# Second attention without the identity and bias products

## The chip, the cores and the metric

The kernel runs on one core of one Trainium2 chip. The metric is the device time of one execution in microseconds (us), less is better. TensorE, VectorE (DVE in the profile), ScalarE (ACT), GpSimd (POOL) and SyncE (SP, which only issues DMAs here) run their own instruction streams and meet at semaphores.

## The reference

Two transformer layers over x of 8 x 512 rows of 256. Each adds an attention and a mixture of experts to the rows, both from one layer norm. The first attention is a causal softmax, the second a gated linear recurrence. What matters here is the end of the second attention, `y @ Wout.T + bout`, which is added to the residual rows:

```python
xn = _layernorm(x, axis=-1)
x = x + _L1_attn_ref(xn, ...) + _L1_ffn_ref(xn, ...)

# in _L1_attn_ref
def step(M, inp):
    q_t, k_t, v_t, f_t, g_t, o_t = inp
    M = M * f_t[..., None, None] + g_t[..., None, None] * scale * (k_t[..., :, None] * v_t[..., None, :])
    y_t = jnp.einsum('bhd,bhde->bhe', q_t, M) * o_t[..., None]
    return (M, y_t)
_, yT = jax.lax.scan(step, M0, (qT, kT, vT, fT, gT, oT))
y = yT.transpose(1, 0, 2, 3).reshape(Bq, Lq, HID)
return jnp.einsum('bld,ed->ble', y, Wout) + bout
```

## The kernel before

The 4096 rows are 32 tiles of 128, kept in SBUF as `ACC` (tile i is `ACC[:, i, :]`, 128x256 f32), eight batches of four tiles. The residual rows stay in `ACC` from start to end; every part of a layer adds to them.

The work after the first layer's experts follows one written-out order, `plan2 = shared_order() + second_order()`. Each engine walks it and does the steps that have code on it. In `shared_order` the remaining products of the first layer's shared part run on TensorE (`shared_up`, L1562; `shared_down`, L1608), and `BEHIND` hangs the second layer's preparation behind them: GpSimd adds loaded sums (`sums`, L1001; `combine`, L1011), VectorE takes the statistics (`stats`), ScalarE normalizes a batch out of `ACC` into `xn1` (`norm`, which signals `xn_made`), TensorE transposes it (`xt`), ScalarE copies it out (`xa`).

`second_order` runs the second attention, one tile per turn, in the order of `ORDER1` (the first tile of each of the 8 batches, then the second of each, and so on). `TURN` gives the steps of a turn and by how many tiles each runs ahead or behind; from the 9th tile on `LATE` moves `weigh`, `out_copy` and `decay_load` to the end. Per tile n:

- TensorE: value product of the tile (`project_val`, L1753), query and key product of the next (`project_qk`, L1741), transposes (`turn`, L1769 and, from the 9th tile, L1777), state and sums of the tile before (`keys`, L1813; `update`, L1822 and L1827), affinities of the tile (`affinity`, L1795), and the output of the tile before (`project_out`).
- VectorE: state update (`update`, L2353), scan of the decays (`decay`, L2334), rotation of the next tile (`rope`, L2314; `rope_add`, L2325 and L2326), weighing of the affinities out of PSUM banks 2 to 5 (`affinity`, L2341, which signals `w_put`).
- ScalarE: values times gates (`value`, L1303), copies of the transposes (`turn`, L1310 and L1315), copy of the sums (`update`, L1321, signals `yt_put`), keys times gates (`keys`, L1339), and the copy of the output (`project_out`, L1344).
- GpSimd: opening of the gates (`open_gates`, L1030 and L1036) and the routing's scatter DMAs (L929).
- SyncE: the decays of a tile ahead (`decay_load`, L802) once `w_put` has come for the tile that held its buffer, loads of expert weights (L788), and `store_sums` (L809), a quarter of the rows at a time, once `oe_put` says that their outputs are done.

`project_val` of a tile waits for `w_put` of the tile before it on TensorE (its output shares bank 3 with the affinities). The output of a tile is made whole in PSUM bank 1: an identity matrix times the rows of `ACC` (L1836), two products of `YT` with `WOUT` (L1839), and a product of three rows of ones with the bias, split in three bf16 parts (L1840). `bias_split` (L1041 to L1055) on GpSimd prepares these parts behind `const1`. ScalarE then copies bank 1 over the rows of `ACC` and signals `oe_put`, for which the next output's first product waits. An f32 product has two records in the trace, so the 32 tiles show 64 records for L1836 and 128 for L1839.

After the last tile TensorE waits for `oe_put` and goes on to the second layer's experts; VectorE's first step there is the copy of an expert's weights (`weights`, L2186), then of the turned rows (`tile_turn`, L2174).

Of the kernel before, what the change touches and what calls it, by code (L numbers as in the profile page):

```python
# [15 lines left out]
T = NB * S  # L16
# [76 lines left out]
def attention_order():  # L93
# [10 lines left out]
    for idx in range(-LEAD, NH + 7):  # L104
# [82 lines left out]
        ("sums_copy", -1), ("project_out", -1), ("keys", 0), ("weigh", 0), ("out_copy", -1), ("rope_add", 1),  # L187
# [4 lines left out]
    (-1, "out_copy"): "scale:7 norm:7",  # L192
# [5 lines left out]
    (0, "out_copy"): "logitsT:7",  # L198
# [7 lines left out]
LATE = [s for s in TURN if s[0] not in ("weigh", "out_copy", "decay_load")] + [("weigh", 0), ("out_copy", -1), ("decay_load", 2)]  # L206
# [25 lines left out]
def second_order():  # L232
# [19 lines left out]
    out += [("rows",)] + [(kind, NT - 1) for kind in ("update", "sums_copy", "project_out", "out_copy")]  # L252
# [47 lines left out]
def build(nc, t, out):  # L300
    ctx = ExitStack()
    with ctx:
        def sem(name):
            return ctx.enter_context(nc.semaphore(name))
# [138 lines left out]
        BO3 = view(carve(128), 128, BF16)  # L443
        ones3 = view(carve(64), 64, BF16)
# [120 lines left out]
        stk_set, v_set = sem("stk_set"), sem("v_set")  # L565
# [11 lines left out]
        b_in, b_cut, b_rows, b_set = sem("b_in"), sem("b_cut"), sem("b_rows"), sem("b_set")  # L577
# [10 lines left out]
        none_set, slot_in, slot_turned, slot_off, slot_put = (sem(n) for n in ("none_set", "slot_in", "slot_turned", "slot_off", "slot_put"))  # L588
# [27 lines left out]
        out_made, oe_put, sums_out = (sem(n) for n in ("out_made", "oe_put", "sums_out"))  # L616
# [28 lines left out]
        def sync(sp):  # L645
# [50 lines left out]
            def maxrow(n):  # L696
# [3 lines left out]
                sp.wait_ge(stk_set, 3)  # L700
# [9 lines left out]
            def clear(p):  # L710
                sp.wait_ge(cst_in, 32)
                sp.wait_ge(none_set, 4)
# [41 lines left out]
            sp.wait_ge(b_cut, 5)  # L754
            sp.wait_ge(b_set, 1)
# [118 lines left out]
        def gpsimd(pool):  # L874
# [5 lines left out]
            for v in Vb:  # L880
                pool.memset(v, 0.0).then_inc(v_set)
            pool.wait_ge(v_set, 2)
            for v in Vb:
                pool.memset(v[:, :, :, 16:17], 1.0).then_inc(v_set)
            pool.wait_ge(v_set, 4)
            for n in range(3):
                if n:
                    pool.wait_ge(stk_set, n)
                pool.memset(STK[n][1][96:99, :, :].rearrange("p j s -> p (j s)").bitcast(F32), ONES2).then_inc(stk_set)
            pool.wait_ge(stk_set, 3)  # L890

            def clear_meta():
                for n, apart in enumerate((128, 0)):
                    pool.memset(unused[n][0:NTILE, :, :], 0.0).then_inc(none_set)
                    pool.wait_ge(none_set, 2 * n + 1)
                    pool.iota(unused[n][0:NTILE, :, 1], [[1, 128]], base=T, channel_multiplier=apart, allow_small_or_imprecise_dtypes=True).then_inc(none_set)
                pool.wait_ge(none_set, 4)
# [11 lines left out]
            def bias_rows():  # L909
                pool.memset(B2S, 0.0).then_inc(b_set)  # L910
                pool.wait_ge(b_in, 32)
                for k in range(3):
                    if k:
                        pool.wait_ge(b_cut, 2 * k)
                    pool.tensor_copy(b3[0:8, k, :], bstage[0:8, :]).then_inc(b_cut)
                    if k < 2:
                        pool.wait_ge(b_cut, 2 * k + 1)
# [120 lines left out]
            def bias_split():  # L1038

                pool.wait_ge(const1_set, 2)  # L1040
                pool.memset(ones3, 0.0).then_inc(const1_set)  # L1041
                for k in range(3):
                    pool.wait_ge(const1_set, 3 + k)
                    pool.memset(ones3[32 * k:32 * k + 1, :], 1.0).then_inc(const1_set)
                pool.wait_ge(const1_set, 6)
                pool.tensor_copy(BO3, BO).then_inc(const1_set)
                pool.wait_ge(const1_set, 7)
                pool.tensor_tensor(BO, BO, BO3, ALU.subtract).then_inc(const1_set)
                for k in (1, 2):
# [1422 lines left out]
```

## Time and profile before

Three runs of the kernel took 1669.58, 1671.32 and 1675.81 us. The profiled execution has a span of 1669.4 us from its first instruction to its last; its time outside the span isn't listed.

| | us |
|---|---|
| median of the runs | 1671.32 |
| span of the profiled execution | 1669.4 |
| TensorE busy | 1569.7 (94%) |
| VectorE busy | 823.6 (49%) |
| ScalarE busy | 734.2 (44%) |
| GpSimd busy | 714.7 (43%) |
| mean granted TensorE clock, share of full | 0.984 |

In time order: the first attention, the first layer's experts until about 785 us, the shared products with the second layer's preparation until about 890, the second attention until about 1131, and the second layer's experts to the end. A row of a timeline gives the start in us from the span's start, the duration in us, the engine, the line of the kernel and the operation. In brackets stands how long the engine sat idle before it and what released it. "PEld" is TensorE's weight load, which runs beside its products. "x4" at the end merges four instructions.

### The profile page before, as it was taken

The numbers are of one execution on the slowest core, as the hardware profiler recorded it, in microseconds if no ns is written. First come the engines' busy times: TensorE is split into PE (matmuls) and PEld (weight loads), VectorE is DVE, ScalarE is ACT, GpSimd is POOL, SyncE is SP. The second block draws the span as 40 slices with busy tenths as digits, with TensorE's granted clock in tenths as the row PEclk, the third lists the DMA queues.
The fourth block names the chain that finished last, engine by engine and source line by source line (L and its number), as shares of the span: only waits on it lengthen the run. The fifth ranks groups of instructions, "written<-read, shape, count | busy, mean of one in ns | idle before, by whom it ended". The sixth has DMA issues, their size and how long they took to land.

```text
span 1669.4 us, 32480 instructions
## 1 busy us (share of the span) xinstructions
PE 1569.7 (94%) x11054; PEld 1210.1 (72%) x11054; DVE 823.6 (49%) x2298; ACT 734.2 (44%) x1923; POOL 714.7 (43%) x815
## 2 busy tenths in 40 slices
PE   6989989999999999999997799988999999999997
PEld 3545445555548999998664567768999999999996
DVE  6867898787812223221477788873221122222220
ACT  4544545555541222222566466644333233333332
POOL 3122336666523555553810467752333333333332
PEclk9989999999999999999999999999999999999999
DMA  8534325534305222222621396466222222222221
GB/s 269 131 103 110 79 70 105 106 91 103 67 17 230 73 70 72 72 70 88 216 103 65 102 221 99 78 123 259 33 38 39 33 39 39 34 37 39 34 38 23
DMA packets 86093, 151.07 MB, mean 90 GB/s; under 512 B 16276, under 2 KB 64272, under 8 KB 82864
## 3 DMA queue, kind: packets, MB, share of 16 engines
q1 hardware_dynamic: 61392, 111.62, 25.3%
q0 software_dynamic: 24544, 37.38, 10.3%
q8 instruction: 96, 1.57, 0.4%
q14 instruction: 61, 0.50, 0.1%
HBM read 104.10 MB, written 44.45 MB: 89 GB/s over the span
## 4 chain that ended last, share of the span: by engine, by line
PE 79%; DVE 9%; DMA 4%; issue 3%; ACT 3%; SPq 1%; POOL 0%; another core or an unknown queue 0%; DVEq 0%; ACTq 0%; POOLq 0%
PE PS L1634 23%; PE PS L1652 22%; PE PS L1491 4%; PE PS L1427 3%; DVE PS L1954 3%; PE PS L1741 3%; PE PS L1476 3%; PE PS L1455 2%; PE PS L1608 2%; PE PS L1562 2%; PE PS L1619 2%; PE PS L1517 2%; PE PS L1437 2%; PE PS L1753 1%; DMA arena<-FD 1%
## 5 line engine op out<-in xcount | busy, mean ns | idle before, releaser
L1634 PEld LDWEIGHTS PS<-arena 128*128 128x128 f32 x3408 | 396.6, 192 | 15.8 <-DVE arena L2174 4.6
L1634 PE MATMUL PS<-arena 128*128 128x128 f32 x3408 | 403.8, 275 | 3.2 <-DVE arena L2174 3.2
L1652 PE MATMUL PS<-arena 128*128 x1704 | 392.4, 379 | 0.0
L1652 PEld LDWEIGHTS PS<-arena 128*128 128x128 f32 x1704 | 311.7, 190 | 40.2 <-issue 0.2
L2174 DVE COPY arena<-PS 128x256 f32<-128x256 f32 x142 | 60.3, 425 | 414.8 <-PE PS L1619 404.2
L1954 DVE CUSTOM_DVE_ANT_0 PS<-PS,arena 128x512 f32<-128x512 f32 (+3 forms) x512 | 235.5, 523 | 46.1 <-PE PS L1455 42.4
L970 POOL DMA_INDIRECT out<-arena x71 | 111.8, 1574 | 313.1 <-ACT arena L1246 292.4
L1236 ACT ACTIVATE arena<-PS,arena 128x128 f32<-128x128 f32 x568 | 162.3, 369 | 137.6 <-PE PS L1634 137.5
L1246 ACT ACTIVATE arena<-PS,arena 128x256 f32<-128x256 f32 x142 | 67.4, 474 | 283.1 <-PE PS L1654 191.3
L903 POOL TENSOR_SCALAR_AFFINE_SELECT arena<-arena 128x256 f32<-128x256 f32 x256 | 100.0, 414 | 207.9 <-ACT arena L1152 207.5
L1152 ACT ACTIVATE arena<-PS 128x512 f32<-128x512 f32 (+1 forms) x256 | 166.3, 704 | 49.9 <-PE PS L1476 40.3
L956 POOL DMA_INDIRECT arena<-XN,arena x142 | 144.4, 1017 | 93.8 <-PE PS L1619 51.9
L929 POOL DMA_INDIRECT SLOT<-arena x128 | 156.1, 1220 | 30.2 <-issue 30.2
L2186 DVE COPY arena<-arena 128x1024 f32 (+1 forms) x142 | 136.7, 963 | 61.7 <-ACT arena L1228 57.9
L963 POOL DMA_INDIRECT SUM<-arena x71 | 70.3, 990 | 111.6 <-ACT arena L1246 105.0
L1455 PE MATMUL PS<-arena 96*128 96x512 bf16 (+3 forms) x512 | 99.8, 307 | 6.0 <-DVE arena L1954 5.8
L1476 PE MATMUL PS<-arena 99*128 99x512 bf16 (+3 forms) x512 | 98.0, 308 | 5.7 <-ACT arena L1152 4.8
L1228 ACT ACTIVATE arena<-PS 128x512 f32<-128x512 f32 x71 | 42.4, 597 | 113.9 <-PE PS L1634 108.4
L1476 PEld LDWEIGHTS PS<-arena 99*128 99x128 bf16 x512 | 45.6, 99 | 57.8 <-issue 20.2
L1455 PEld LDWEIGHTS PS<-arena 96*128 96x128 bf16 x512 | 49.2, 99 | 46.6 <-DVE arena L1954 16.3
L1491 PE MATMUL PS<-arena 128*32 128x512 f32 (+3 forms) x1024 | 75.7, 435 | 4.5 <-DVE arena L1940 3.6
L2334 DVE TENSOR_TENSOR_SCAN arena<-arena 128x1024 f32<-128x1024 f32 x32 | 73.1, 2286 | 7.6 <-DMA arena<-FD 7.5
(246 smaller groups left out, 1985.6 us busy)
## 6 DMA issues: line engine op xcount, KB each, us to landing
arena<-FD SPq DMA_DIRECT2D x32, 512.0 KB
arena<-in_w SPq DMA_DIRECT2D x16, 1024.0 KB
SPL<-arena SPq DMA_DIRECT2D x32, 384.0 KB, 2.6
arena<-SPL SPq DMA_DIRECT2D x64, 192.0 KB
XN<-arena SPq DMA_DIRECT2D x16, 512.0 KB, 3.2
arena<-SPL SPq DMA_DIRECT2D x64, 128.0 KB
arena<-SUM SPq DMA_DIRECT2D x16, 512.0 KB, 6.4
arena<-in_x SPq DMA_DIRECT2D x8, 512.0 KB, 6.4
```

Of the source, the lines that this page charges most:

```text
L929: pool.indirect_dma_start(SLOT[layer], bass.IndirectOffsetOnAxis(ap=POS[:, n, i:i + 1], axis=0), META[:, i, n, :], None).then_inc(row_out[ ...
L956: pool.indirect_dma_start(MOE[layer].xr[i % 4][:, :], None, XN, row).then_inc(tile_in[i % 4], 16)
L970: pool.indirect_dma_start(out, row, m.y[i % 3][:, :], None, compute_op=ALU.add).then_inc(y_out[i % 3], 16)
L1152: act.activation(PB[h % NPB][:, lo:hi], ps(3, lo, hi), ACT.Exp, scale=0.25).then_inc(p_made)
L1236: ins = act.activation(m.hT[i % len(m.hT)][:, 128 * f:128 * f + 128], ps(m.UPB[i % 2], 128 * f, 128 * f + 128), ACT.Gelu, bias=m.bias[i % ...
L1455: ins = pe.matmul(ps(0, o, o + w), q[0:96, j, 128 * i:128 * i + 128], k[0:96, j, 0:w], start=True, stop=True)
L1476: ins = pe.matmul(ps(3, o, o + w), k[0:99, j, 128 * kb:128 * kb + 128], q[0:99, j, 128 * kb:512], start=True, stop=True)
L1491: ins = pe.matmul(PS[32 * j:32 * j + 32, 6, 128 * kb:512], vb[:, kb, 8 * half + jj, :], PB[(8 * n + jj) % NPB][:, OFFT[kb]:OFFT[kb] + w], ...
L1634: ins = pe.matmul(o, m.now[i % 2][:, c * F + 128 * f:c * F + 128 * f + 128], m.xt[i % 2][:, 128 * c:128 * c + 128], start=(c == 0), stop=( ...
L1652: ins = pe.matmul(to, m.hT[i % len(m.hT)][:, 128 * c:128 * c + 128], m.WD[:, bass.ds(e * (nf * 256) + c * 256, 256)], start=(c == 0), stop ...
L1954: dve.tensor_tensor_reduce(sc, sc, MASK[:, 384 - 128 * r:512], -1.0, -NEG, ALU.add, ALU.min, NM[n % 2][:, r, j:j + 1]).then_inc(s_max)
L2186: dve.tensor_copy(m.now[i % 2][:, :], m.WU[:, bass.ds(e * m.wrow, m.wrow)]).then_inc(w_staged)
```

## The change

The identity product and the bias product go, and with them `bias_split`, its tiles `BO3` and `ones3`, and ScalarE's copy of the output. GpSimd adds the bias to the four tiles of a batch in `ACC` at the step `xa`, once ScalarE has made the normalized rows from them. VectorE adds the two remaining products out of PSUM to the rows (`out_add`), which signals `oe_put`. In `TURN` the step `out_copy` becomes `out_add` and moves behind `rope_add`; in `LATE` it keeps its place behind `weigh`. Some semaphores that count one-time setup are merged (`stk_set` and `v_set` into `pads_set`, `none_set` into `const_set`, `b_set` into `b_cut`).

```diff
@@ TURN, AMONG, LATE
-        ("sums_copy", -1), ("project_out", -1), ("keys", 0), ("weigh", 0), ("out_copy", -1), ("rope_add", 1),
+        ("sums_copy", -1), ("project_out", -1), ("keys", 0), ("weigh", 0), ("rope_add", 1), ("out_add", -1),
-LATE = [s for s in TURN if s[0] not in ("weigh", "out_copy", "decay_load")] + [("weigh", 0), ("out_copy", -1), ("decay_load", 2)]
+LATE = [s for s in TURN if s[0] not in ("weigh", "out_add", "decay_load")] + [("weigh", 0), ("out_add", -1), ("decay_load", 2)]
@@ gpsimd
-            def bias_split():
...
+            def bias_add(b):
+                pool.wait_ge(xn_made, b + 1)
+                four = ACC[:, 4 * b:4 * b + 4, :]
+                pool.tensor_tensor(four, four, BO.unsqueeze(1).to_broadcast([128, 4, 256]), ALU.add).then_inc(bo_put)
...
                 elif kind == "const1":
                     const1()
-                    bias_split()
+                elif kind == "xa":
+                    bias_add(*a)
@@ scalar
-            def project_out(n):
-                act.wait_ge(out_made, n + 1)
-                act.activation(ACC[:, ORDER1[n], :], ps(1, 256, 512), ACT.Copy).then_inc(oe_put)
@@ tensor
                 if n:
                     pe.wait_ge(oe_put, n)
-                else:
-                    pe.wait_ge(const1_set, 12)
-                pe.matmul(ps(1, 256, 512), ident, ACC[:, ORDER1[n], :], start=True, stop=False)
                 pe.wait_ge(yt_put, n + 1)
                 for g in range(2):
-                    pe.matmul(ps(1, 256, 512), YT[:, 128 * g:128 * g + 128], WOUT[:, g, :], start=False, stop=False)
-                pe.matmul(ps(1, 256, 512), ones3[0:96, :], BO3[0:96, :], start=False, stop=True).then_inc(out_made)
+                    ins = pe.matmul(ps(1, 256, 512), YT[:, 128 * g:128 * g + 128], WOUT[:, g, :], start=(g == 0), stop=(g == 1))
+                ins.then_inc(out_made)
@@ vector
+            def out_add(n):
+                i = ORDER1[n]
+                dve.wait_ge(bo_put, min(n + 1, NB))
+                dve.wait_ge(out_made, n + 1)
+                dve.tensor_tensor(ACC[:, i, :], ps(1, 256, 512), ACC[:, i, :], ALU.add).then_inc(oe_put)
```

## Rows read from the trace of the kernel before

**Rows 1.** Stretches: us, busy PE, PEld, DVE, ACT, POOL; clock; DMA share; GB/s.

```profile
780.00:870.00 90.00, 86.82 (x428) 58.59 (x427) 44.27 (x176) 52.28 (x85) 42.08 (x32) 0.98 0.51 166
...
890.00:955.00 65.00, 51.35 (x480) 33.34 (x479) 53.00 (x77) 39.03 (x151) 16.70 (x14) 0.92 0.25 71
955.00:1060.00 105.00, 102.41 (x1079) 71.70 (x1077) 84.37 (x99) 69.60 (x287) 76.19 (x70) 1.00 0.70 155
...
916.00:923.00 7.00, 6.21 (x69) 4.07 (x68) 6.90 (x10) 5.33 (x22) 0.93 (x1) 1.00 0.20 75
```

**Rows 2.** Timeline of TensorE's products, one steady tile of the second attention.

```profile
998.17 1.10 PE L1753 MATMUL PS<-arena 128*128 128x256 f32 x4
...
1003.71 0.70 PE L1836 MATMUL PS<-arena 128*128 128x256 f32 x2
1004.25 1.03 PE L1839 MATMUL PS<-arena 128*128 128x256 f32 x4
1005.11 0.27 PE L1840 MATMUL PS<-arena 96*128 96x256 bf16 x1
1005.22 1.10 PE L1753 MATMUL PS<-arena 128*128 128x256 f32 x4
```

**Rows 3.** Timeline of VectorE, the same tile.

```profile
1001.10 1.23 DVE L2314 TENSOR_TENSOR arena<-PS,arena 128x1024 f32<-128x1024 f32 x1 [0.36 <-PE PS L1741]
...
1003.85 1.23 DVE L2341 TENSOR_TENSOR arena<-PS,arena 128x1024 f32<-128x1024 f32 x1 [0.63 <-PE PS L1795]
1004.99 0.60 DVE L2353 SCALAR_TENSOR_TENSOR arena<-arena,PS 128x128 f32<-128x128 f32 x2
```

**Rows 4.** Timeline of all engines, a tile in which L1753 waited for the weighing.

```profile
989.74 1.22 DVE L2341 TENSOR_TENSOR arena<-PS,arena 128x1024 f32<-128x1024 f32 x1
...
991.07 0.73 PEld L1753 LDWEIGHTS PS<-arena 128*128 128x128 f32 x4 [1.82 <-issue]
991.10 1.10 PE L1753 MATMUL PS<-arena 128*128 128x256 f32 x4 [1.46 <-DVE arena L2341]
```

**Rows 5.** Timeline of all engines: ScalarE's copy, and the weight load of L1753.

```profile
1003.28 0.38 ACT L1321 ACTIVATE arena<-PS 128x256 f32<-128x256 f32 x1 [0.94 <-PE PS L1827]
...
1005.19 0.30 PEld L1753 LDWEIGHTS PS<-arena 128*128 128x128 f32 x2 [0.19 <-issue]
```

**Rows 6.** Timeline of all engines, a late tile.

```profile
1080.90 1.23 DVE L2341 TENSOR_TENSOR arena<-PS,arena 128x1024 f32<-128x1024 f32 x1 [0.17 <-PE PS L1795]
...
1082.27 1.10 PE L1753 MATMUL PS<-arena 128*128 128x256 f32 x4
```

**Rows 7.** VectorE's groups by line, 500 to 1131: busy us, mean ns.

```profile
L2353 DVE SCALAR_TENSOR_TENSOR arena<-arena,PS 128x128 f32<-128x128 f32 x32 | 9.6, 340 | 0.0
L2165 DVE TENSOR_TENSOR arena<-PS,arena 128x512 f32<-128x512 f32 x14 | 9.4, 684 | 21.7 <-PE PS L1608 21.7
```

**Rows 8.** Timelines of TensorE and VectorE, where the early stretch ends.

```profile
933.70 1.66 PE L1753 MATMUL PS<-arena 128*128 128x256 f32 x4 [4.77 <-DVE arena L2341]
...
938.32 1.23 DVE L2314 TENSOR_TENSOR arena<-PS,arena 128x1024 f32<-128x1024 f32 x1 [1.04 <-PE PS L1741]
```

**Rows 9.** GpSimd and VectorE timelines, and L1030 by line: ns min/median/max.

```profile
838.53 2.36 POOL L1011 TENSOR_TENSOR arena<-arena 128x1024 f32<-128x1024 f32 x1 [7.98 <-DVE arena L2165]
...
934.99 2.29 DVE L2334 TENSOR_TENSOR_SCAN arena<-arena 128x1024 f32<-128x1024 f32 x1
...
935.15 2.53 POOL L1030 TENSOR_TENSOR arena<-arena 128x256 f32<-128x256 f32 x1 [10.36 <-DVE arena L2326]
...
L1030 POOL TENSOR_TENSOR arena<-arena x32: 611/613/2532, 880.0 to 1118.2; 128x256 f32<-128x256 f32 x32
```

**Rows 10.** Timeline of all engines, the end of the second attention.

```profile
1126.79 1.23 DVE L2186 COPY arena<-arena 128x2048 f32 x1
...
1129.90 0.38 ACT L1344 ACTIVATE arena<-PS 128x256 f32<-128x256 f32 x1 [1.33 <-PE PS L1840]
...
1130.83 0.42 DVE L2174 COPY arena<-PS 128x256 f32<-128x256 f32 x1 [2.82 <-PE PS L1619]
```

More of the change, by code:

```diff
@@ L191 @@
     (-1, "keys"): "root:7",
-    (-1, "out_copy"): "scale:7 norm:7",
+    (-1, "out_add"): "scale:7 norm:7",
     (0, "turn"): "xt:7",
@@ L197 @@
     (0, "weigh"): "gates:1:0",
-    (0, "out_copy"): "logitsT:7",
+    (0, "out_add"): "logitsT:7",
     (0, "rope_add"): "logitsT_copy:7",
@@ L251, in second_order @@
             out.append(("slots",))
-    out += [("rows",)] + [(kind, NT - 1) for kind in ("update", "sums_copy", "project_out", "out_copy")]
+    out += [("rows",)] + [(kind, NT - 1) for kind in ("update", "sums_copy", "project_out", "out_add")]
     return out
@@ L587, in build @@
         r_pos = sem("r_pos")
-        none_set, slot_in, slot_turned, slot_off, slot_put = (sem(n) for n in ("none_set", "slot_in", "slot_turned", "slot_off", "slot_put"))
+        slot_in, slot_turned, slot_off, slot_put = (sem(n) for n in ("slot_in", "slot_turned", "slot_off", "slot_put"))
         row_out = [sem(f"row_out{n}") for n in range(4)]
@@ L615, in build @@
         kd_put, y_made, yt_put, dm_made, m_put = (sem(n) for n in ("kd_put", "y_made", "yt_put", "dm_made", "m_put"))
-        out_made, oe_put, sums_out = (sem(n) for n in ("out_made", "oe_put", "sums_out"))
+        out_made, bo_put, oe_put, sums_out = (sem(n) for n in ("out_made", "bo_put", "oe_put", "sums_out"))
         xt_ready = {b: [(banks0[f"xt{c}", b][0], banks0[f"xt{c}", b][1] + 1) for c in range(2)] for b in range(NB)}
@@ L699, in maxrow @@
                 sp.wait_ge(s_made, 24 * n + 24)
-                sp.wait_ge(stk_set, 3)
+                sp.wait_ge(pads_set, 7)
                 if n >= 3:
@@ L711, in clear @@
                 sp.wait_ge(cst_in, 32)
-                sp.wait_ge(none_set, 4)
+                sp.wait_ge(const_set, 7)
                 if p == 0:
@@ L752, in sync @@
                     slots(0)
-            sp.wait_ge(b_cut, 5)
-            sp.wait_ge(b_set, 1)
+            sp.wait_ge(b_cut, 6)
             for k in range(3):
@@ L880, in gpsimd @@
             for v in Vb:
-                pool.memset(v, 0.0).then_inc(v_set)
-            pool.wait_ge(v_set, 2)
+                pool.memset(v, 0.0).then_inc(pads_set)
+            pool.wait_ge(pads_set, 2)
             for v in Vb:
-                pool.memset(v[:, :, :, 16:17], 1.0).then_inc(v_set)
-            pool.wait_ge(v_set, 4)
+                pool.memset(v[:, :, :, 16:17], 1.0).then_inc(pads_set)
+            pool.wait_ge(pads_set, 4)
             for n in range(3):
                 if n:
-                    pool.wait_ge(stk_set, n)
-                pool.memset(STK[n][1][96:99, :, :].rearrange("p j s -> p (j s)").bitcast(F32), ONES2).then_inc(stk_set)
-            pool.wait_ge(stk_set, 3)
+                    pool.wait_ge(pads_set, 4 + n)
+                pool.memset(STK[n][1][96:99, :, :].rearrange("p j s -> p (j s)").bitcast(F32), ONES2).then_inc(pads_set)
+            pool.wait_ge(pads_set, 7)
             def clear_meta():
                 for n, apart in enumerate((128, 0)):
[L894 to L897, printed above, removed]
+                    pool.memset(unused[n][0:NTILE, :, :], 0.0).then_inc(const_set)
+                    pool.wait_ge(const_set, 2 * n + 4)
+                    pool.iota(unused[n][0:NTILE, :, 1], [[1, 128]], base=T, channel_multiplier=apart, allow_small_or_imprecise_dtypes=True).then_inc(const_set)
+                pool.wait_ge(const_set, 7)
             def future(h):
@@ L1129, in project_v @@
                 act.wait_ge(v_made, 2 * b + half + 1)
-                act.wait_ge(v_set, 4)
+                act.wait_ge(pads_set, 4)
                 if b >= 2:
@@ L2382, in vector @@
                     update(*a)
+                elif kind == "out_add":
+                    out_add(*a)
                 elif kind == "route":
```

31 lines of the change are left out of this document (5 added, 26 removed).

## The prediction

> **What bounds the kernel now.** I read the stretches first [rows 1]. The change lives in two of them. From 780 to 870 us the shared products of the first layer's tail run and TensorE is busy 86.82 of 90 us; only the bias work on GpSimd moves here. From 890 to 1130 the second attention runs its 32 tiles. From 955 to 1060 TensorE is busy 102.41 of 105, which looks like an engine-bound loop from which every product removed is time won. Between 890 and 955 it is busy 51.35 of 65, VectorE 53.00.
>
> The busy share hides a second limit, so I followed one tile of the steady part on TensorE [rows 2] and on VectorE [rows 3]. Its order on TensorE: the affinities (L1795), the identity product (L1836), the two output products (L1839), the bias product (L1840), then the value product of the next tile (L1753). That last one waits in its code for `w_put`, the end of VectorE's weighing (L2341), since both use bank 3. The reader is to see two clocks that meet. TensorE's own work from the start of L1836 to that of L1753 is 1005.22 - 1003.71 = 1.51 us. VectorE starts the weighing at 1003.85, ends at 1005.08, and a product that surely waited for it started 0.14 after such an end (989.74 + 1.22 = 990.96, started at 991.10 [rows 4]). 1005.08 + 0.14 = 1005.22, the same instant. The weight load of L1753 says which holds it: it begins at 1005.19 after 0.19 idle [rows 5], 1.34 after the weighing began; in the tile that surely waited it is 1.33 (991.07 - 989.74). I compared the two starts in all tiles from the 9th to the 30th: 1.33 to 1.35 in each. In one of them the weighing began 0.11 instead of 0.14 after L1836, and the load moved with the weighing. A late tile, where the state updates are gone, has the same distance from weighing to L1753, 1082.27 - 1080.90 = 1.37 against 1005.22 - 1003.85 = 1.37 [rows 2, 3, 6].
>
> So the loop is L1753, about 5.5 us of products, L1795, the weighing, L1753: 1005.22 - 998.17 = 7.05 us [rows 2]. L1836 and L1840 lie wholly in the shadow of the weighing.
>
> **TensorE's part.** Removed per tile: L1836, 1004.25 - 1003.71 = 0.54 on the path, and L1840, 1005.22 - 1005.11 = 0.11. In all 32 x 0.65 = 20.8 us of TensorE work, but the release of L1753 stays at 1005.22: worth 0 in the 24 tiles from the 9th on. L1839 starts sooner, after L1795 and ScalarE's copy of the sums (L1321, ends 1003.66 [rows 5]), and ends near 1004.8; TensorE then idles about 0.4 us. In the first eight tiles one L1753 starts 0.2 later than its weighing would allow, since ScalarE's copy came late and L1840 stood behind it; I credit -0.2 in all.
>
> **VectorE's part.** Added: 32 x out_add, 128x256, one operand in PSUM. No row has that form. 128 columns take 340 ns (L2353) and 512 take 684 (L2165) [rows 7], which interpolates to 455 at 256; the next instruction starts 0.09 before such an end (1004.99 against 1005.08 [rows 3]), so it occupies 0.37. Ends: 0.25 (L2353 less the overlap) and 0.59 (L2165 less the overlap). In the steady part it goes behind the weighing, ahead of the update and the scan. VectorE idles 0.36 ahead of L2314 and 0.63 ahead of L2341 in each tile [rows 3], 0.99 in all. The first hole takes all but 0.01 of the 0.37, the second the rest; the weighing starts when it did. Its new wait, for `out_made`, has the update, the scan and the next rotation queued behind it; with the last L1839 done near 1004.8 and the weighing near 1005.0 it waits for nothing. Cost 0; with both holes gone it would be 0.37 in each of the 24 tiles, 8.9 us.
>
> The first tiles are different. From the 2nd to the 6th, VectorE also does the gates and the routing, and is the bound: busy 6.90 of 7.00 us in one stretch [rows 1], and the stretch ends with a weighing that releases L1753 at 933.70 after 4.77 us of waiting [rows 8]. Ahead of that weighing stand four out_adds (tiles 0 to 3), each 0.37: +1.5. The fifth falls into the 1.04 hole ahead of L2314 at 938.32 [rows 8]. If the holes of the routing chain took some of them it would be 0.8; if all seven of the early order cost 0.45 it would be 3.2.
>
> **ScalarE's part.** 32 copies (L1344) go, 0.38 us each [rows 10]. ScalarE isn't on the loop: 0.
>
> **GpSimd's part.** Eight additions of 128x1024 come, 2.36 us each by the same shape in L1011 [rows 9], 19 us; the bias split goes (about 4 us of small instructions). They stand at the `xa` steps, where TensorE itself has already waited for the same `xn_made`, so the wait adds none. Queued behind them are `sums`, `combine` and the opening of the gates. By the times of the queue the pair for batches 0 and 1 replaces the split ahead of the 4th combine and moves it by under 1 us; the rest fall into GpSimd's waits, 7.98 us ahead of the combine at 838.53 and longer ones after [rows 9]. Without that cover each would cost its 2.4. Cost 0, ends 0 and +3.
>
> When GpSimd's opening of the gates (L1030, 613 ns by its median) starts just behind a scan on VectorE (935.15 behind 934.99), it takes 2.53 us [rows 9]: one of the two shut the other out. The Trainium skill, "SBUF — State Buffer", section "Who interferes with whom", says why and adds the other direction: a VectorE instruction with two SBUF inputs and a GpSimd one that reads SBUF share a port, whoever starts first keeps it, and the other blocks fully. The trace agrees in the one direction. By that rule the new additions can hold up VectorE, which is the third rival.
>
> **The end.** The last output goes 1129.90 + 0.38 by ScalarE now [rows 10]. Without L1836 and L1840 the last L1839 ends 0.5 to 0.7 sooner. But VectorE now must do the last out_add before it copies the first expert's weights, 1.2 us, which it did at 1126.79 in idle time [rows 10]. Out_add to about 1129.6, weights to about 1130.9, then the turned rows that were copied at 1130.83: 0.1 later than now. I take 0; ends -0.7 and +0.4.
>
> **Sum.** +1.5 - 0.2 + 0 + 0 = +1.3 us. The profiled span is 1669.4; the median of the runs, 1671.3, is 1.9 above it. 1669.4 + 1.3 + 1.9 = 1672.6 us.
>
> **Rivals.** *TensorE is the bound after all* (the meeting of the two clocks is chance and L1753 doesn't need the weighing). Then a steady tile falls to the longer of TensorE, 7.05 - 0.65 = 6.40, and VectorE, 7.05 - 0.99 + 0.37 = 6.43: 0.62 less in 23 tiles, -14.3, and with +1.3 the time is 1658.3. For it: 102.41 of 105 busy. Against: the code's wait, the load's idle 0.19 and the equal 1.34. Chance 0.11.
>
> *VectorE becomes the bound*: out_add comes late in every tile, because the output products finish after the weighing and the scan stands behind it. It decides from 0.99 - 0.37 = 0.62 us of lateness; at 1.0 us of it each tile costs 0.38, over 31 tiles +11.8: 1671.3 + 11.8 + 1.3 = 1684.4. For it: a strict order with nothing between. Against: the near 1004.8. Chance 0.06.
>
> *GpSimd's additions hold VectorE up.* By row times two of the eight meet such an instruction; if each held the stretch by its whole 2.4, +4.8: 1677.4. If all eight did, +19: 1692. Against: TensorE bounds that stretch. Chances 0.04 and 0.02.
>
> *The clock*: TensorE gets holes of 0.3 to 0.7 us per tile. The stretch 916 to 923 had it busy 6.21 of 7.00 at a granted clock of 1.00 [rows 1], so I give it no case of its own.
>
> **How the numbers follow.** Forecast 0.77, with its own range 1666 to 1679: the ends of the terms, -0.1 to +6.4 in all against now, and the 6 us by which the runs of before differ. The rest: 1658.3 at 0.11, 1684.4 at 0.06, the additions 0.06. Stretching 2 us to either side for the near parts of the rivals gives 1664 to 1681. A measurement of this kernel can tell about 0.5%, 8.4 us. Faster by more than that 0.13, same 0.78, slower 0.09.
>
> **What would show it.** Right: steady tiles still 7.05 us apart, L1753 now marked as waiting about 0.4 us for VectorE, out_add without a wait of its own, VectorE's idle time per tile down by 0.37, the L1753 that starts at 933.70 about 1.5 later, clock 1.00. Wrong: tiles of 6.4 to 6.6 us, out_add waiting on L1839, two-input instructions of VectorE lengthened between 840 and 884, or a clock under 1.00 after 955.

## The result and the profile after

| | before | after |
|---|---|---|
| median of the runs, us | 1672.53 (1668.71 to 1677.62, 18 runs) | 1679.36 (1672.11 to 1686.17, 18 runs) |
| ratio after / before | | 1.0036 [1.0021, 1.0051] |
| span of the profiled execution, us | 1669.4 | 1670.3 |
| mean granted TensorE clock | 0.984 | 0.984 |

The change costs 0.36% of 1672.53, 6.0 us; by its interval 3.5 to 8.5 (the two medians are 6.8 apart). The forecast was a loss too small to tell, at +1.3 us. It is a loss, 0.36% by its middle, but the size is not the forecast's: some 5 us are missing. The profiled execution of after is its fastest (1672.11 us) and shows little of them by its span, so the loss has to be looked for in stretches with fixed work.

The stretches of after that answer to [rows 1] (us, busy PE, PEld, DVE, ACT, POOL, then clock, DMA share, GB/s):

```profile
780.00:870.00 90.00, 84.36 (x423) 55.72 (x421) 49.11 (x187) 51.85 (x82) 53.79 (x29) 0.98 0.53 167
890.00:955.00 65.00, 46.19 (x457) 29.93 (x456) 54.44 (x82) 35.58 (x137) 13.79 (x14) 0.86 0.28 68
955.00:1060.00 105.00, 98.55 (x1038) 65.66 (x1036) 90.80 (x114) 65.20 (x277) 74.86 (x70) 0.99 0.65 156
```

TensorE lost 3.9 us of work in the stretch from 955 to 1060 and VectorE got 6.4 more, and the steady tiles are as far apart as before. One steady tile, TensorE and then VectorE (affinities L1772, output products L1813, next value product L1730; weighing L2315, out_add L2321, update L2333, scan L2308):

```profile
974.88 0.73 PE L1772 MATMUL PS<-arena 32*128 32x128 f32 x16
975.54 1.12 PE L1813 MATMUL PS<-arena 128*128 128x256 f32 x4
977.04 1.10 PE L1730 MATMUL PS<-arena 128*128 128x256 f32 x4 [0.38 <-DVE arena L2315]
```

```profile
975.67 1.23 DVE L2315 TENSOR_TENSOR arena<-PS,arena 128x1024 f32<-128x1024 f32 x1 [0.44 <-PE PS L1772]
976.81 0.42 DVE L2321 TENSOR_TENSOR arena<-PS,arena 128x256 f32<-128x256 f32 x1
977.14 0.60 DVE L2333 SCALAR_TENSOR_TENSOR arena<-arena,PS 128x128 f32<-128x128 f32 x2
...
982.72 1.23 DVE L2315 TENSOR_TENSOR arena<-PS,arena 128x1024 f32<-128x1024 f32 x1 [0.63 <-PE PS L1772]
```

The value product now waits 0.38 us for the weighing, 1.37 us after that began, as in [rows 2, 3]. The next weighing comes 7.05 us later (982.72 - 975.67). The steady part is as forecast.

The end of the attention is not. Below is after's TensorE, then its VectorE (L1596 turns an expert tile's rows, L1611 is the expert's first product, L2160 copies its weights, L2148 the turned rows):

```profile
1126.73 1.10 PE L1813 MATMUL PS<-arena 128*128 128x256 f32 x4 [1.41 <-issue]
1128.46 0.41 PE L1596 MATMUL PS<-arena 128*128 128x128 f32 x2 [0.63 <-issue]
1130.66 0.41 PE L1596 MATMUL PS<-arena 128*128 128x128 f32 x2 [1.78 <-DVE arena L2148]
1130.90 8.94 PE L1611 MATMUL PS<-arena 128*128 128x128 f32 x64
```

```profile
1123.29 1.23 DVE L2315 TENSOR_TENSOR arena<-PS,arena 128x1024 f32<-128x1024 f32 x1 [0.94 <-PE PS L1772]
...
1127.94 0.43 DVE L2321 TENSOR_TENSOR arena<-PS,arena 128x256 f32<-128x256 f32 x1 [3.09 <-PE PS L1813]
...
1128.95 1.23 DVE L2160 COPY arena<-arena 128x2048 f32 x1
1130.10 0.42 DVE L2148 COPY arena<-PS 128x256 f32<-128x256 f32 x1
```

The same place in the kernel before, whose last weighing began at 1125.55 (L1619 turns, L1634 is the first expert product):

```profile
1130.38 0.41 PE L1619 MATMUL PS<-arena 128*128 128x128 f32 x2 [0.52 <-issue]
1131.40 0.41 PE L1619 MATMUL PS<-arena 128*128 128x128 f32 x2 [0.61 <-DVE arena L2174]
1131.65 7.31 PE L1634 MATMUL PS<-arena 128*128 128x128 f32 x64
```

Before: 1131.65 - 1125.55 = 6.10 us from the last weighing to the first expert product, and 7.31 for the first 64 products. After: 1130.90 - 1123.29 = 7.61 and 8.94. That is 3.1 us in one place. The weights' copy (1.23 us), which before ran at 1126.79 [rows 10] in idle time, now queues behind the last out_add, which waits 3.09 us for its product; TensorE idles 1.78 us between its two turns (0.61 before), and over 10 us from about the first turn its granted clock is 0.83, a mean of its two levels (1.2 and 2.4 GHz), and not 1.00:

```profile
1130.55:1140.55 10.00, 8.82 (x77) 8.38 (x77) 3.94 (x7) 5.75 (x17) 3.46 (x3) 1.00 0.97 344
```

```profile
1128.29:1138.29 10.00, 8.04 (x56) 7.87 (x57) 3.31 (x7) 3.60 (x10) 3.63 (x2) 0.83 0.91 318
```

The first is the kernel before, the second after. The experiments stand in the order in which they ran, and their first theories are not this one; it came only when thirteen profiles could be laid side by side.

### The profile page after: what moved, and what is told of

It reads as the page before. It is cut to its first block and busy times, and to the rows that moved or that the text cites. A ratio compares the mean times of both kernels' runs of the same rounds, so it can differ in the third digit from the quotient of the medians.

```text
span 1670.3 us, 32347 instructions
## 1 busy us (share of the span) xinstructions
PE 1551.3 (93%) x10958; PEld 1195.5 (72%) x10958; DVE 838.7 (50%) x2330; ACT 722.1 (43%) x1891; POOL 726.7 (44%) x813
## 5 line engine op out<-in xcount | busy, mean ns | idle before, releaser
L1611 PEld LDWEIGHTS PS<-arena 128*128 128x128 f32 x3408 | 399.9, 193 | 15.8 <-DVE arena L2148 4.5
L1611 PE MATMUL PS<-arena 128*128 128x128 f32 x3408 | 407.0, 276 | 3.1 <-DVE arena L2148 3.1
L2148 DVE COPY arena<-PS 128x256 f32<-128x256 f32 x142 | 60.3, 425 | 412.2 <-PE PS L1596 401.8
L2160 DVE COPY arena<-arena 128x1024 f32 (+1 forms) x142 | 136.6, 962 | 63.3 <-ACT arena L1211 60.9
L2308 DVE TENSOR_TENSOR_SCAN arena<-arena 128x1024 f32<-128x1024 f32 x32 | 74.0, 2311 | 1.7 <-DMA arena<-FD 1.7
```

What stands on the lines that cost most here:

```text
L1611: ins = pe.matmul(o, m.now[i % 2][:, c * F + 128 * f:c * F + 128 * f + 128], m.xt[i % 2][:, 128 * c:128 * c + 128], start=(c == 0), stop=( ...
L2160: dve.tensor_copy(m.now[i % 2][:, :], m.WU[:, bass.ds(e * m.wrow, m.wrow)]).then_inc(w_staged)
```

## The experiments

Ratios are to the kernel before, on the same chip. The lines of the experiments' kernels are a few off those of before and after. Each run has one profile, so what a profile shows is one execution. FD is the DRAM tensor from which the decay blocks are loaded.

**1. The changed kernel again.**

> The changed kernel, unaltered, once more. The profiled execution shown so far (1670.3 us) is one of the shortest of its 18 runs; their median is 1679.4 against 1672.5 before. Theory A (placement): the rest of the difference is lost time in the first tiles of the second attention, where VectorE is the bound; then the stretch 870 to 961 takes longer and all steady tiles stay at 7.05 us. Theory B (clock): the holes that the removed products leave on TensorE let its granted clock fall for some stretch in most runs, so that the mean clock of a run goes with its time, and a steady tile shows a clock under 1.00 and over 7.05 us. I expect 1676 to 1682 us. A single execution near 1670 would decide nothing.

Measured: 1679.27 us, ratio 1.0027 [1.0010, 1.0044], span 1680.2. The loss is real; together with the first comparison it is 4.5 to 6 us. Its profile held a surprise in the stage ahead of the attention. VectorE's tiny multiply-add of the third batch's scale (L2205, 0.16 us where nothing holds it) took 5.13 us, while GpSimd ran two of the new additions (L1038) and the copy behind them (L1012). First VectorE, then GpSimd:

```profile
812.62 0.16 DVE L2205 SCALAR_TENSOR_TENSOR arena<-arena 128x4 f32<-128x4 f32 x1
...
820.16 5.13 DVE L2205 SCALAR_TENSOR_TENSOR arena<-arena 128x4 f32<-128x4 f32 x1
```

```profile
819.60 4.66 POOL L1038 TENSOR_TENSOR arena<-arena 128x1024 f32<-128x1024 f32 x2
824.20 0.10 POOL L1011 MEMSET arena<- 128x2 f32 x1
824.24 1.03 POOL L1012 COPY arena<-arena 128x1024 bf16<-128x1024 bf16 x1
```

820.16 + 5.13 = 825.29, the end of the copy (825.27). This is the third rival's mechanism. The Trainium skill, "SBUF — State Buffer", section "Who interferes with whom", gives the rule for it, and here the trace agrees with the other direction, GpSimd first. The prediction had found only the one direction in the trace of before, but the other is there too. The same multiply-add took 0.80 us at 819.64 and ended at 820.44, beside a GpSimd addition that ended at 820.42:

```profile
819.64 0.80 DVE L2231 SCALAR_TENSOR_TENSOR arena<-arena 128x4 f32<-128x4 f32 x1
```

```profile
818.06 2.36 POOL L1011 TENSOR_TENSOR arena<-arena 128x1024 f32<-128x1024 f32 x1
```

New in experiment 1 is that it was held over two additions and a copy, not over one instruction.

**2. TensorE's part alone.**

```diff
-                pe.matmul(ps(1, 256, 512), ident, ACC[:, ORDER1[n], :], start=True, stop=False)
...
-                pe.matmul(ps(1, 256, 512), ones3[0:96, :], BO3[0:96, :], start=False, stop=True).then_inc(out_made)
+                ins.then_inc(out_made)
```

> The kernel before without the identity and the bias product alone; ScalarE's copy and GpSimd's bias split stay. Leaves out the residual rows and the output bias of the second attention. Theory of the prediction (both products lie in the shadow of VectorE's weighing): steady tiles stay 7.05 us apart, 0 to -1 us in all. Rival (TensorE is the bound): 6.4 us per tile, -14 us. Theory B (clock): this kernel has TensorE's holes and none of the other edits, so it is 2 to 6 us slower than before.

Measured: ratio 0.9989 [0.9971, 1.0007], nearly all steady tiles 7.04 to 7.05. Both products are worth nothing that can be measured, and taking them away alone costs at most 0.07% (1.2 us), not the 2 to 6 us of theory B. The clock itself did fall more: 0.97 from 955 to 1060, where before has 1.00. What that can cost stands behind experiment 12.

**3 and 4. The query and key product ahead of the value product, in the changed kernel and in the kernel before.**

```diff
-TURN = [("state", -2), ("route", 0), ("project_val", 0), ("project_qk", 1), ("turn", 0),
+TURN = [("state", -2), ("route", 0), ("project_qk", 1), ("project_val", 0), ("turn", 0),
```

> The changed kernel with one pair of steps exchanged in each turn: TensorE makes the query and key product of the next tile ahead of the value product, so that the product that waits for VectorE's weighing has 1.7 us of other work in front of it. Theory of the prediction: the loop through the weighing opens, and a steady tile falls from 7.05 to the longer of TensorE (6.40) and VectorE (6.43), about -14 us in 23 tiles, and less than the full sum in the first eight, so 1663 to 1668 us. If the weighing isn't what holds the tile, 0.

> The same exchange in the kernel before. There TensorE's own work of a tile is as long as the loop through the weighing, so by the theory of the prediction the tile stays at 7.05 us: 0, with up to -2 in the tiles where the weighing came late. If an exchange gained as much here as in the changed kernel, the removed products would have nothing to do with it.

Measured: 1.0010 [0.9990, 1.0030] with steady tiles of mostly 6.85 (five of fifteen about 7.3, mean 7.01), and 1.0022 [1.0007, 1.0038] with 7.39 to 7.40. Both sizes missed. With 1.88 us of another product between, the value product no longer waits for the weighing; TensorE waits for ScalarE instead, whose values (L1286) come later and hold up its copies (L1293, L1298). TensorE and ScalarE of the swapped changed kernel:

```profile
1015.90 1.88 PE L1718 MATMUL PS<-arena 128*128 128x512 f32 x4
1017.62 1.03 PE L1730 MATMUL PS<-arena 128*128 128x256 f32 x4
1021.12 0.73 PE L1772 MATMUL PS<-arena 32*128 32x128 f32 x16 [0.35 <-ACT arena L1298]
```

```profile
1018.68 1.54 ACT L1286 ACTIVATE arena<-PS,arena 128x32 f32<-128x32 f32 x8 [2.61 <-PE PS L1730]
1020.06 0.65 ACT L1293 ACTIVATE arena<-PS 128x512 f32<-128x512 f32 x1
1020.53 0.45 ACT L1298 ACTIVATE arena<-PS 128x256 f32<-128x256 f32 x1
```

7.39 - 6.85 = 0.54 has the size of the identity product, as if it counts once the weighing's shadow is gone, and not before. That would be the shadow of the forecast, seen from its other side. It is a match of sizes and not shown: the two kernels differ by the whole change, and by the mean of 7.01 the difference is 0.38.

**5 and 6. GpSimd's part alone (the bias product goes with it), VectorE's part alone**, in the kernel before.

```diff
-                    bias_split()
+                elif kind == "xa":
+                    bias_add(*a)
```

> The kernel before with one part of the change alone: the output bias is added to the rows by GpSimd's eight additions, where the change puts them, and the bias product on TensorE and the cutting of the bias rows are gone; the product with the identity, ScalarE's copy and the plan stay. Theory (GpSimd's additions hold up VectorE's instructions that read two tiles from SBUF): the additions carry the loss, so this is slower than the kernel before by 3 to 6 us (ratio 1.002 to 1.0035), and the profile shows the 128x128 multiply-add before the second combine batch at about 2.3 us, as in the three kernels with the additions, and not at 0.29. Rival 1 (VectorE's out_add carries the loss): within 1 us of before. Rival 2 (a lower clock because TensorE does less): the bias product was worth 0.3 us a tile, so within 1 us here as well.

```diff
-                elif kind == "out_copy":
-                    project_out(*a)
...
+            def out_add(n):
+                i = ORDER1[n]
+                dve.wait_ge(out_made, n + 1)
+                dve.tensor_tensor(ACC[:, i, :], ps(1, 256, 512), ACC[:, i, :], ALU.add).then_inc(oe_put)
```

> The kernel before with the other part alone: VectorE reads the output product from PSUM and adds the rows, in the place that the change gives it; the identity and bias products, GpSimd's work and the plan's rest stay (the rows go in twice, since the identity product stays). Theory: out_add costs what the early tiles show, 4 additions of about 0.4 us, and nothing in the steady tiles (7.05 us apart as before): +1 to +2 us (ratio 1.001). The 128x128 multiply-add keeps 0.29 us. Rival 1 (out_add carries the loss): +4 to +7 us (ratio 1.003 to 1.004), with steady tiles over 7.1.

Measured: 1.0027 [1.0004, 1.0049] and 1.0018 [0.9999, 1.0038]. The multiply-adds were held up as expected with GpSimd's part (4.45 us and 2.33 us) and not with VectorE's (0.29 us for the second). But VectorE's part came to 3 us where the theory had 1 to 2, which left something open. The intervals overlap, so these two do not split the loss by themselves.

**7. VectorE's addition without the identity product, the bias left on TensorE.**

```diff
-                pe.matmul(ps(1, 256, 512), ident, ACC[:, ORDER1[n], :], start=True, stop=False)
...
-                    pe.matmul(ps(1, 256, 512), YT[:, 128 * g:128 * g + 128], WOUT[:, g, :], start=False, stop=False)
+                    pe.matmul(ps(1, 256, 512), YT[:, 128 * g:128 * g + 128], WOUT[:, g, :], start=(g == 0), stop=False)
```

> The change without its GpSimd part: VectorE adds the rows to the output product and the identity product is gone, but the bias stays a product on TensorE and GpSimd cuts the bias rows as before. Theory: the change's +6 us less what GpSimd's additions cost, so +1 to +2 us against before (ratio 1.0005 to 1.0015), steady tiles 7.05 apart. Rival 1 (out_add): +4 to +7 us. Rival 2 (the clock falls because TensorE has less to do in a tile): nearly all of the work taken from TensorE is still taken (0.24 of 0.54 us a tile), so +2 to +4 us.

Measured: 1.0027 [1.0010, 1.0045], +4.5 us where the theory had +1 to +2 and the first rival +4 to +7. No addition on GpSimd, and yet most of the loss by its middle; the interval reaches down to +1.7. So VectorE's part likely carries more than the early tiles.

**8. A version meant to beat both.** The old way for the first eight tiles, then VectorE's addition, and in the late tiles the turn split in two.

```diff
+LATE = [("state", -2), ("route", 0), ("turn_q", 0), ("turned_q", 0), ("project_val", 0), ("project_qk", 1), ("turn_e", 0), ("value", 0), ("turned_e", 0),
...
+                if n < NB:
+                    pe.matmul(ps(1, 256, 512), ident, ACC[:, ORDER1[n], :], start=True, stop=False)
```

> A version meant to beat both. In the first eight tiles the second attention's output goes the way of the kernel before (identity product, ScalarE's copy), where VectorE sets the end; from the ninth tile on VectorE adds the rows and the identity product is gone; the bias stays on TensorE; no additions on GpSimd. In the late tiles the first part of the turn (q) stands ahead of project_val, and its copy on ScalarE too, so that the chain weighing to weighing loses one product and one copy. From the swap of the changed kernel (6.85 us a tile against 7.05) and the 0.19 us that its chain still waited on ScalarE: steady tiles of 6.6 to 6.8, over 17 tiles 4 to 8 us, and none of the early loss: ratio 0.995 to 0.998. If a wait I do not see closes the chain again: 7.05 a tile and a ratio of 1.000.

Measured: steady tiles 6.60 to 6.62 us apart, as hoped, and a ratio of 1.0036 [1.0012, 1.0060]. The gain of 0.44 us a tile doesn't reach the time. In the profile the scans wait 13.9 us in all for the decay blocks from DRAM (`FD`), against 7.5 us before. That this is what takes the gain isn't shown: experiments 5 and 12, with tiles of 7.05, wait 12.4 and 13.7 us in theirs.

```profile
985.26 2.29 DVE L2352 TENSOR_TENSOR_SCAN arena<-arena 128x1024 f32<-128x1024 f32 x1 [4.52 <-DMA arena<-FD]
993.12 2.29 DVE L2352 TENSOR_TENSOR_SCAN arena<-arena 128x1024 f32<-128x1024 f32 x1 [1.58 <-DMA arena<-FD]
...
1099.28 2.29 DVE L2352 TENSOR_TENSOR_SCAN arena<-arena 128x1024 f32<-128x1024 f32 x1 [6.41 <-DMA arena<-FD]
```

**9. The additions held back.**

```diff
                 pool.wait_ge(xn_made, b + 1)
+                if b < 2:
+                    pool.wait_ge(normed, 22)
+                elif b == 5:
+                    pool.wait_ge(gate_d, 3)
```

> The changed kernel, with three of GpSimd's eight additions held back until VectorE is past the instruction that they block: the first two wait for the scale of the third batch (a 128x4 multiply-add), the sixth for the gates' 128x128 multiply-add. Nothing else differs. Theory (the loss is VectorE waiting behind GpSimd's additions): the multiply-adds take at most 1 us and 0.29 us, where the kernels with free additions showed 1.03, 1.14, 4.45 and 5.13 us for the one and 2.33 us for the other four times; from the first batch's scale to the first weighing 71 us as without additions, where free additions showed 71.9, 72.0, 77.1 and 78.2; time against before +1 to +3 us (ratio 1.0005 to 1.002), that is 3 to 5 us less than the change. Rival (the late start of the attention has another cause, the lower clock at 820 to 850): 72 to 78 us as before and a ratio of 1.003 to 1.0036.

Measured: ratio 1.0041 [1.0021, 1.0061]. The profile did what the edit meant: 71.41 us from the first batch's scale to the attention's first rotation, the longest such multiply-add behind the first batch's (1.6 us in every kernel) is 1.10 us, and the second kind is back at 0.29:

```profile
818.42 1.10 DVE L2209 SCALAR_TENSOR_TENSOR arena<-arena 128x4 f32<-128x4 f32 x1
...
854.71 0.29 DVE L2271 SCALAR_TENSOR_TENSOR arena<-arena 128x128 f32<-128x128 f32 x1
```

The time did not. The theory that this hold is most of the loss has its range, up to 1.002, just below the interval.

**10. The additions in four pieces each.**

```diff
-                pool.tensor_tensor(four, four, BO.unsqueeze(1).to_broadcast([128, 4, 256]), ALU.add).then_inc(bo_put)
+                for i in range(4 * b, 4 * b + 4):
+                    if i:
+                        pool.wait_ge(bo_put, i)
+                    pool.tensor_tensor(ACC[:, i, :], ACC[:, i, :], BO, ALU.add).then_inc(bo_put)
```

> The changed kernel with each of GpSimd's eight additions (128x1024, 2.35 us) cut into four of one tile (128x256, some 0.6 us), each waiting for the one before it, so that GpSimd leaves a gap after every 0.6 us. Theory (VectorE's multiply-add waits for a gap in GpSimd's instructions, and two additions in a row left none): no multiply-add over 1.3 us; from the first batch's scale to the first weighing 71 to 72.5 us; ratio 1.0005 to 1.0025. Rival (VectorE is held as long as GpSimd has work queued, gap or not): 4 to 5 us as before in about half of the executions, and a ratio as the change's, 1.003 to 1.0036.

Measured: no multiply-add over 1.24 us behind the first batch's, as the mechanism says, 72.73 us in the same stretch (71 to 72.5 expected), and a ratio of 1.0051 [1.0027, 1.0075], which again speaks against the hold as the cause of the time.

**11. The weights' loads spaced**, on the version of experiment 8.

```diff
-                    if a[0] >= 8 and early:
+                    if a[0] >= 8 and a[0] % 2 == 0 and early:
```

> The version with the turn split in the late tiles (e8_hybrid_turn), whose steady tiles were 6.61 us apart but which waited 13.9 us in all for the decay blocks from DRAM, with one difference: the one-megabyte loads of the experts' weights, one in each tile from the ninth on, now go with every second tile. Theory (the shorter tiles are given back because the decay blocks arrive late beside the weights): the two waits near 985 and 993 (6.1 us together) go or shrink under 2 us, those near 1087 and 1099 stay, since no weights are loaded there: 3 to 6 us less than e8_hybrid_turn, ratio to before 0.999 to 1.001. Rival (the late blocks are slow in themselves): waits of the same sum elsewhere, ratio 1.002 to 1.005.

Measured: the waits near 985 and 993 gave way to two of 1.30 and 1.29 us, those at the end stayed (1.88 and 4.67), as expected; but the ratio is 1.0053 [1.0034, 1.0072]. One tile took 12.64 us and the next 9.00, both free of waits for `FD`; the trace names no releaser of this core for the first, and the second ran at a clock of 0.50 (1042 to 1048). Spacing the loads doesn't win the time back. That it removed the early waits is likely but not shown, since after has no such wait ahead of 1097 with the loads unspaced.

**The end of the attention, in all thirteen profiles.** With all of them at hand I measured three stretches in each. The end fell into two groups, by which engine writes the last tile's output:

| last output by | kernels | last weighing to first expert product | first 64 products | from there to the end |
|---|---|---|---|---|
| ScalarE's copy | before, 2, 4, 5 | 6.10, 5.75, 6.43, 5.88 | 7.31 in each | 537.75, 537.91, 538.05, 538.07 |
| VectorE's addition | after, 1, 3, 6, 7, 8, 9, 10, 11 | 7.61, 8.27, 7.85, 7.30, 7.06, 7.46, 7.85, 6.70, 8.11 | 8.94, 8.58, 9.41, 8.94, 9.94, 8.42, 8.47, 8.94, 8.92 | 539.25 to 540.38, mean 539.61 |

The means are 6.04 and 7.58, and 537.95 and 539.61: 1.5 + 1.7 = 3.2 us, without an overlap. From TensorE's first turn to the first expert product the groups are further apart: 1.27 us in each of the four, 2.42 to 2.98 in the nine. Experiment 6, which has every product of before, is in the second group, and 2, which lacks two of them, in the first, so the cause is the addition, not missing TensorE work.

**12. The weights' copy ahead of the last addition**, on experiment 9.

```diff
                 elif kind == "out_add":
+                    if a[0] == NT - 1:
+                        dve.wait_ge(wu_in, 192)
+                        dve.wait_ge(r_expert, 2)
+                        dve.wait_ge(b1_put, 1)
+                        weights(1, 0)
                     out_add(*a)
```

> e9_ordered with one move: VectorE's copy of the first expert tile's weights (128x2048, 1.2 us) stands ahead of the last tile's addition of the output product, and not behind it. New theory, from the thirteen traces so far: in the nine kernels whose last tile goes by VectorE's addition, that addition waits some 3 us for the last output product, the copy queues behind it and lands on the path to the first expert product; the product starts 6.7 to 8.3 us after the last weighing and the first 64 products take 8.4 to 9.9 us at a lower clock; in the four kernels whose last tile goes by ScalarE's copy it is 5.75 to 6.43 us and 7.31 us. Expected if that is so: first expert product 5.6 to 6.6 us after the last weighing, the first 64 products 7.31 us, from the first of them to the end 537.7 to 538.1 us against 539.3 to 540.4; ratio to before 1.0005 to 1.0025, that is 3 us under e9_ordered's 1.0041. Left then is what the early tiles cost, 1.6 us, and 0.4 us in the stage before. Rival (the tail is long because the copy's place follows from something else, as VectorE's PSUM read of the last product): 7 to 8 us and 8.9 us as in e9_ordered, ratio 1.0035 to 1.0045.

Measured: ratio 1.0018 [0.9998, 1.0038], and the end is that of the first group. Last weighing at 1130.23, then on VectorE:

```profile
1132.53 1.23 DVE L2164 COPY arena<-arena 128x2048 f32 x1
1134.05 0.42 DVE L2326 TENSOR_TENSOR arena<-PS,arena 128x256 f32<-128x256 f32 x1 [0.29 <-PE PS L1817]
1135.13 0.42 DVE L2152 COPY arena<-PS 128x256 f32<-128x256 f32 x1 [0.65 <-PE PS L1600]
```

and on TensorE:

```profile
1134.58 0.41 PE L1600 MATMUL PS<-arena 128*128 128x128 f32 x2 [0.63 <-issue]
1135.69 0.41 PE L1600 MATMUL PS<-arena 128*128 128x128 f32 x2 [0.70 <-DVE arena L2152]
1135.94 7.31 PE L1615 MATMUL PS<-arena 128*128 128x128 f32 x64
```

5.71 us to the first expert product, 7.31 for the first 64, and 1673.6 - 1135.94 = 537.66 to the end. 1.36 us lie between the first turn and the first product. Order alone moves it, with the addition still reading the last product from PSUM; the rival is out. That is the profile. In time the step from experiment 9 (1.0041) fits the 3 us, but the two intervals overlap. The clock recovers with the wait: over 10 us from 1135.23 it is granted at 1.00.

```profile
1135.23:1145.23 10.00, 8.97 (x78) 8.77 (x79) 3.73 (x7) 5.75 (x17) 3.46 (x3) 1.00 1.01 361
```

**The clock behind a wait, in all fourteen profiles.** A second thing goes with the missing products. From the ninth weighing to the last, the four profiles that keep the identity product in these tiles (before, 4, 5, 6) have the clock at 1.00 throughout, though TensorE stands still for up to 3.31 us in them. Of the ten without it, nine have one to three stretches at 0.50 (1.2 GHz), each of 3.4 to 6.8 us, behind waits of 1.6 to 5.8 us; the profile of after has none. Experiment 12 after a late decay block, then experiment 5 with the identity product (L1734 and L1739 are the value product, L1722 and L1727 the query and key product):

```profile
988.00:994.00 6.00, 3.70 (x7) 2.34 (x8) 5.16 (x8) 1.54 (x8) 4.43 (x4) 0.50 0.91 287
990.30 2.04 PE L1734 MATMUL PS<-arena 128*128 128x256 f32 x4 [4.74 <-DVE arena L2320]
992.14 3.02 PE L1722 MATMUL PS<-arena 128*128 128x512 f32 x4
```

```profile
993.00:999.00 6.00, 2.69 (x19) 2.01 (x12) 5.27 (x8) 2.04 (x9) 2.06 (x3) 1.00 0.99 210
997.97 1.10 PE L1739 MATMUL PS<-arena 128*128 128x256 f32 x4 [3.31 <-DVE arena L2326]
998.91 1.88 PE L1727 MATMUL PS<-arena 128*128 128x512 f32 x4
```

In experiment 12 the next weighing came 9.08 us after the one at 988.94, and not 7.05: 2 us for one such stretch. The waits aren't of the same length, and experiment 2 is not slower than before, so this stays a likely part of what the removed products cost, and no run isolates it.

No version here beats the kernel before.

## Why the prediction was right and where it was not

- **Steady tiles, 0 us: right, and shown.** 7.05 us apart after as before; the 0.38 wait of the value product was forecast as about 0.4. Experiment 2 shows the products worth nothing; 3 and 4 fit with 0.54 as soon as the shadow is gone. "TensorE is the bound after all" is refuted.
- **out_add's duration and place: right.** The row says 0.42 us, and the next instruction starts 0.33 or 0.34 later, against 0.37 forecast. "VectorE becomes the bound" did not come: in the tile shown it waits for nothing, in nine others 0.17 to 0.36, and only in the last 3.09.
- **Early tiles, +1.5 us: right in kind, a third too large.** I compared the time from the second weighing to the seventh. One interval in it takes 12.2 to 12.4 or 13.4 to 13.7 us in kernels of either kind, so like goes with like: 48.01 and 47.94 (before, 8) against 49.19 and 49.28 (1, 9) is +1.3; 49.61, 49.56, 49.56 (2, 5, 11) against 50.41, 50.14, 50.58, 50.69, 50.34 (after, 6, 7, 10, 12) is +0.85. The wait of L1753 in [rows 8] went from 4.77 to 5.73, 0.96 more, at 936.35.
- **The end, "I take 0; ends -0.7 and +0.4": the step that failed.** It measured +3.2, shown by experiment 12 in its profile. The prediction named the right thing, the weights' copy behind the last out_add, and mispriced it twice. First, it had the last product end 0.5 to 0.7 us sooner, so that the copy would still fit. In after, the last product ended 4.54 us after the start of the last weighing (1126.73 + 1.10 - 1123.29), and TensorE turned the first expert tile at 5.17, against 4.83 before: no earlier. The copy then stood on the path nearly whole: 2.44 us from first turn to first product against 1.27. Second, it gave TensorE's clock no case of its own, on the ground of a busy stretch in the middle of the attention. At the end TensorE stands still for 1.78 us, and its next 64 products cost 8.94 and not 7.31. The stretches at 0.50 in the steady tiles (behind experiment 12) are a second place where this ground did not hold.
- **GpSimd, "Cost 0, ends 0 and +3": too low, size open.** The third rival's mechanism exists, and the sign that the prediction named for it came: in after the 128x128 multiply-add of the gates took 2.33 us at 852.65, against 0.29 before. From that multiply-add to the attention's first rotation it is 21.87 to 21.97 us in the seven kernels without the additions, 23.20 or 23.21 in the four with free ones, and 22.35 to 22.64 in 9, 10 and 12: up to 1.3 us are GpSimd's. From the first batch's scale to the attention's first rotation (which the expectations call, wrongly, the first weighing) it is 70.87 to 71.01 us in five kernels without the additions (before, 2, 4, 6, 8; 71.98 in 7 and 69.30 in 11), and with free additions 71.94 and 72.03 where VectorE got in first (3, after), 77.12 and 78.15 where GpSimd did (5, 1). So in that stretch it costs 1 us or 6 to 7, by who comes first. Held back, 71.41 and 72.42 (9, 12), and in pieces 72.73 (10). In time, though, experiment 9 is no faster than the changed kernel. Either the long hold is rare over the executions or it is absorbed later, by the waits for `FD`, which range from 0 to 13.9 us from profile to profile. The runs don't settle which. That it costs nothing is not shown either: experiment 5 has, beside the additions, only the missing bias product, and its ratio is 1.0027 with a lower end at 1.0004.
- **The sum.** End 3.2, early tiles 1, the stage before it 1, steady 0: 5.2 us, without a long hold and without the steady tiles' stretches at 0.50. Measured 6.0 (3.5 to 8.5). Experiment 12, without the end's part, has 3.0 (-0.3 to +6.3).

The forecast was inside 0.5% because all its terms are small beside 8.4 us, not because the last one was right. That part is luck. The measured 1679.36 lies inside the stated 1664 to 1681, whose upper end was stretched for the rivals, but 0.4 above the forecast's own 1666 to 1679. That upper end doesn't follow from its working: the terms alone reach 1671.3 + 6.4 = 1677.7, which leaves 1.3 us for runs that differ by 6. And the measurement tells 2.5 us to either side, not 8.4, so the loss is clear of it.

## What to carry to other kernels

Work that moves to an engine takes its place in that engine's queue at the seams too: look at the last instance, what is queued behind it, and which idle time the queue's next item has used until now. A wait that costs 1.2 us where TensorE restarts costs the clock's part on top. A product in the shadow of another engine's instruction is worth nothing while the shadow lasts (experiment 2). An engine's removed work can also be what kept its clock up over a wait: compare the granted clock behind each wait, not only the mean.

## What the hardware showed that I had not expected

- A multiply-add of 128x4 with two SBUF inputs (0.16 us) took 4.45 and 5.13 us behind two GpSimd additions of 2.35 us queued in a row. In experiment 1 it got in neither between the two nor ahead of the copy that followed. With the additions cut into 0.6 us pieces that wait for one another, the longest was 1.24 us. A boundary between two GpSimd instructions is enough at times: in before it got in at 808.43, between two additions that followed each other without a gap (1.62 us, from 806.84). What decides it, no run here shows.
- It goes by who is first, in both directions. Before, a gate opening on GpSimd took 2.53 us behind a scan [rows 9]. After, out_add let GpSimd start first, and the scan (2.28 us elsewhere) paid, 2.59; all of L1027 take 609 to 632 ns. Timeline of after:

```profile
937.64 0.42 DVE L2321 TENSOR_TENSOR arena<-PS,arena 128x256 f32<-128x256 f32 x1
937.81 0.61 POOL L1027 TENSOR_TENSOR arena<-arena 128x256 f32<-128x256 f32 x1 [11.29 <-DVE arena L2300]
937.98 2.59 DVE L2308 TENSOR_TENSOR_SCAN arena<-arena 128x1024 f32<-128x1024 f32 x1
```

